# Causal mask of the self blocks' scores: added by VectorE in PSUM instead of laid there by TensorE

## The reference

```python
q = _layernorm(q, qln_g, qln_b) * E ** (-0.25)
k = _layernorm(k, kln_g, kln_b) * E ** (-0.25)
dot = jnp.einsum('bihd,bjhd->bhij', q, k)
causal = jnp.triu(jnp.ones((T, T), dtype=bool), k=1)
dot = jnp.where(causal, -jnp.inf, dot)
att = jax.nn.softmax(dot, axis=-1)
out = jnp.einsum('bhij,bjhd->bihd', att, v).reshape(B, T, E)
```

## Time and profile before

| | |
|---|---|
| Time, median of 3 runs | 1171.24 us (1169.45 to 1173.36) |
| Profiled execution: its time | 1169.33 us |
| Profiled execution: its span | 1167.6 us |
| PE busy | 1029.7 us (88%) |
| DVE busy | 724.1 us (62%) |
| ACT busy | 596.7 us (51%) |
| POOL busy | 267.0 us (23%) |
| Row maxima on DVE (L1158) | 256 instructions, 270.1 us |
| Mask strips on PE (L521) | 1024 matmuls, 18.9 us of busy time |

### The profile page before, as it was taken

How to read it: one execution, slowest core, us unless ns; L and a number is a source line. 1 busy time by engine, 2 the same in 40 slices (tenths; PEclk the granted TensorE clock), 3 DMA queues, 4 the chain that set the end, 5 groups by cost and what they waited for, 6 DMA issues and landing times.

```text
span 1167.6 us, 29067 instructions
## 1 busy us (share of the span) xinstructions
PE 1029.7 (88%) x10925; PEld 767.3 (66%) x10925; DVE 724.1 (62%) x1584; ACT 596.7 (51%) x1024; POOL 267.0 (23%) x309
## 2 busy tenths in 40 slices
PE   6899999999999999999999999877189999999930
PEld 3556666666666666666666666545179999999930
DVE  4656666666677877677878787753524444444446
ACT  3567767767755566665555655654122222222225
POOL 1053232232232200000212121132512222222210
PEclk9999999999999999999999999998589999999975
DMA  7117446446441000100101100011267777677656
GB/s 290 29 36 249 149 144 209 147 146 211 142 126 30 12 20 12 47 12 20 40 26 35 34 26 30 13 40 40 92 203 215 219 215 210 213 214 218 202 201 253
DMA packets 95078, 139.25 MB, mean 119 GB/s; under 512 B 11264, under 2 KB 68992, under 8 KB 93920
## 3 DMA queue, kind: packets, MB, share of 16 engines
q1 hardware_dynamic: 88320, 114.98, 31.6%
q0 software_dynamic: 6624, 22.42, 4.9%
HBM read 76.56 MB, written 60.29 MB: 117 GB/s over the span
## 4 chain that ended last, share of the span: by engine, by line
PE 80%; issue 6%; DVE 5%; ACT 3%; DMA 2%; SPq 2%; another core or an unknown queue 0%; ACTq 0%; DVEq 0%; POOLq 0%
PE PS L824 11%; PE PS L561 11%; PE PS L835 11%; PE PS L582 10%; PE PS L531 5%; PE PS L635 5%; PE PS L639 5%; PE PS L706 5%; PE PS L653 4%; PE PS L680 3%; PE PS L538 2%; PE PS L669 2%; PE PS L534 2%; ACT pT L904 2%; PE PS L813 1%
## 5 line engine op out<-in xcount | busy, mean ns | idle before, releaser
L1158 DVE TENSOR_REDUCE part<-PS 128x6 f32<-128x768 f32 (+1 forms) x256 | 270.1, 1087 | 117.9 <-PE PS L538 85.0
L904 ACT ACTIVATE pT<-PS 128x768 f32<-128x768 f32 (+1 forms) x256 | 220.8, 915 | 102.6 <-PE PS L561 89.8
L561 PE MATMUL PS<-big 32*128 32x256 f32 (+1 forms) x2048 | 133.2, 373 | 20.4 <-issue 11.7
L1595 POOL TENSOR_SCALAR_AFFINE_SELECT pT<-pT 128x512 f32<-128x512 f32 x128 | 84.2, 659 | 278.7 <-ACT pT L904 274.9
L824 PEld LDWEIGHTS PS<-oT,big 128*128 128x128 f32 x1136 | 139.8, 194 | 5.4 <-ACT oT L1034 1.8
L824 PE MATMUL PS<-oT,big 128*128 128x128 f32 x1136 | 140.6, 278 | 1.0 <-ACT oT L1034 1.0
L561 PEld LDWEIGHTS PS<-big 32*128 32x128 f32 x2048 | 95.9, 184 | 62.5 <-issue 61.2
L582 PE MATMUL PS<-pT,vaug 128*32 128x256 f32 (+1 forms) x2048 | 125.0, 361 | 13.6 <-DVE sq L1227 3.5
L835 PE MATMUL PS<-w2s,qkn 128*128 x568 | 134.5, 380 | 0.0
L1034 ACT ACTIVATE oT<-PS 128x256 f32<-128x256 f32 x71 | 27.2, 383 | 192.7 <-PE PS L813 192.7
L1615 POOL DMA_INDIRECT xs_dram<-rows_all,posi x64 | 62.1, 971 | 250.1 <-PE PS L531 174.2
(11 more groups left out here) (170 smaller groups left out, 1533.8 us busy)
## 6 DMA issues: line engine op xcount, KB each, us to landing
big<-w SPq DMA_DIRECT2D x71, 512.0 KB
xs_dram<-zrow SPq DMA_DIRECT2D x24, 1496.0 KB, 9.8
oT<-xs_dram SPq DMA_DIRECT2D x71, 136.0 KB
xin<-xT SPq DMA_DIRECT2D x16, 256.0 KB, 2.9
w2s<-w POOLq DMA_DIRECT2D x1, 4096.0 KB, 15.8
xb<-x SPq DMA_DIRECT2D x16, 256.0 KB, 11.2
xin<-ctxT SPq DMA_DIRECT2D x16, 256.0 KB, 2.8
big<-nmaxT SPq DMA_DIRECT2D x128, 4.0 KB
```

The lines of the kernel that those rows point to most:

```text
L561: ins = pe.matmul(o, keys, a[r0:r1, 0, g, q0:T], start=True, stop=True)
L904: act.activation(pT[:, k % 2, 2 * half:2 * half + 2, 0:wide], src, ACT.Exp).then_inc((exp_a, exp_b)[half], 1)
L1158: dve.tensor_reduce(dst, src, AX.X, ALU.max, negate=True).then_inc((max_a, max_b)[half], 1)
L1595: pool.affine_select(d, d, [[0, 2], [0, 2], [1, P]], ALU.is_ge, 0.0, base=0, channel_multiplier=-1).then_inc(masked, 1)
```

## The change

The strips go. TensorE scores self groups like cross groups (`start=True`), and VectorE adds a mask tile `causal` (128x128, fp32, in SBUF) in place onto the diagonal squares in PSUM, one instruction of 128x512 elements for two banks, two for a group, before it takes the maxima. A new semaphore `veiled` counts the adds; each reduction waits for the add of its own half. Both adds stand ahead of the first reduction.

```diff
@@ decoder_block
         ident = sb("ident", [P, P])
-        identb = sb("identb", [P, P], BF16)
-
-        strips = sb("strips", [P, STRIPS, P], BF16)
+
+        causal = sb("causal", [P, P])
...
@@ score(u), TensorE
-                if not cross:
-                    if k == 0:
-                        pe.wait_ge(mask_ready, 1)
-                    for j in range(STRIPS):
-                        for i in range(GRP):
-                            r0, r1 = PADDED * i, PADDED * (i + 1)
-                            diagonal = bank(S_BANK[i])[:, 0:2 * T].rearrange("p (t k) -> p t k", t=2)
-                            pe.matmul(diagonal[:, :, PADDED * j:PADDED * (j + 1)], strips[r0:r1, j, :],
-                                      identb[r0:r1, r0:r1].unsqueeze(1).to_broadcast([PADDED, NT, PADDED]),
-                                      start=(j == 0), stop=False, skip_group_check=True)
...
-                            ins = pe.matmul(o, q, a[r0:r1, 1, g, 0:P], start=False, stop=True,
-                                            skip_group_check=True)
+                            ins = pe.matmul(o, q, a[r0:r1, 1, g, 0:P], start=True, stop=True)
...
@@ TensorE, before the quarters
-            pe.wait_ge(mask_laid, 1)
-            for j in range(STRIPS):
-                ins = pe.transpose(bank(5)[:, j * P:(j + 1) * P], columns4[:, j, :], ident[:])
-            ins.then_inc(mask_pe, 1)
@@ VectorE, before the quarters
-            for i in range(GRP):
-                ins = dve.tensor_copy(columns4[:, :, PADDED * i:PADDED * (i + 1)],
-                                      cst[:, 1, :].rearrange("p (j m) -> p j m", j=STRIPS))
-            ins.then_inc(mask_laid, 1)
...
-            dve.tensor_copy(identb[:], cst[:, 0, :])
+            dve.tensor_copy(causal[:], cst[:, 1, :]).then_inc(veiled, 1)
...
-            dve.wait_ge(mask_pe, 1)
-            dve.tensor_copy(strips[:].rearrange("p j q -> p (j q)"), bank(5)).then_inc(mask_ready, 1)
@@ maxima(u, half), VectorE
                 if half == 0:
                     dve.wait_ge(scores_pe, NG * n + g + 1)
...
+                    if not crossed(n):
+                        if g == 0 and n == 0:
+                            dve.wait_ge(veiled, 1)
+                        for both in S_HALF:
+                            own = both.rearrange("p (i b k) -> p i b k", i=2, k=P)[:, :, 0:3:2, :]
+                            dve.tensor_tensor(own, own, causal[:].unsqueeze(1).unsqueeze(1).to_broadcast([P, 2, 2, P]),
+                                              ALU.add).then_inc(veiled, 1)
+                if not crossed(n):
+                    dve.wait_ge(veiled, 2 * (NG * n + g) + half + 2)
                 src = S_HALF[half].rearrange("p (i c) -> p i c", i=2)
```

More of the change, by code:

```diff
@@ L27 @@
 PADDED = 32
-STRIPS = P // PADDED
 MASKED = -1e30
@@ L260, in decoder_block @@
         wm = pflat[:, 2816:2816 + 64]
-        columns4 = pflat[:, 3072:3072 + 4 * P].rearrange("p (j t) -> p j t", j=STRIPS)
         PS = ctx.enter_context(nc.psum_tensor("PS", [P, 4096], F32))
@@ L273, in decoder_block @@
         ident_ready, centered = sem("ident_ready"), sem("centered")
-        mask_laid, mask_pe, mask_ready = sem("mask_laid"), sem("mask_pe"), sem("mask_ready")
+        veiled = sem("veiled")
         init_link, pool_ready, zrow_ready = sem("init_link"), sem("pool_ready"), sem("zrow_ready")
@@ L533, in score @@
                             o = bank(S_BANK[i])[:, 0:P]
-                            ins = pe.matmul(o, q, a[r0:r1, 1, g, 0:P], start=False, stop=True,
-                                            skip_group_check=True)
+                            ins = pe.matmul(o, q, a[r0:r1, 1, g, 0:P], start=True, stop=True)
                         else:
                             o = bank(S_BANK[i])[:, P:P + T]
-                            ins = pe.matmul(o, q, a[r0:r1, 1, g, :], start=False, stop=True,
-                                            skip_group_check=True)
+                            ins = pe.matmul(o, q, a[r0:r1, 1, g, :], start=True, stop=True)
                 ins.then_inc(scores_pe, 1)
```

## The result

The changed kernel takes 1234.9 us (median of 4 runs, 1225.5 to 1236.7), against 1170.4 for the kernel before in the same series (4 runs, 1169.5 to 1173.4): a ratio of 1.053, with a 95% interval from 1.0472 to 1.0589. The forecast was 1230, slower by 5%. In the profiled executions, on which the sum was made, it is 1233.21 against 1169.33: 63.9 us more, where the sum gave 59.0.

What follows compares the result with a forecast made beforehand. TensorE was taken to bound the kernel, with `score_T` waiting for VectorE's `max_a`. Adds cost 67.3 us, strips give back 8.3, net 59.0 on 1169.33: 1228.3, forecast 1230 us, 5% slower; range 1215 to 1255.

Steps and rivals of the forecast that it cites:

- The place: In self groups, `score_T` needs `max_a`; adds ahead of the first reduction delay that reduction by 1.22 us.
- The price of an add in PSUM: VectorE's mask adds, 128x512: 0.69 us each, starts 0.61 us apart, taken from an add that reads PSUM.
- Rival 1: Adds dearer than a PSUM read: 1.48 us a pair gives 1246 us, 2.4 us about 1303; chance 0.14.
- 2.28 us to `score_T`: From the start of the first add to `score_T`: 1.22 plus 1.06 us, in all four kinds of quarter.
- Quarters 14 to 71: Delay of `score_T`: 36.6 us for 30 quarters without slack, 12.9 with r = 2, 12.0 with r = 3.
- The strips: Removing 16 strip matmuls in each of 64 groups brings scores 0.13 us earlier per group, 8.3 us off.
- Rival 3: VectorE's added work is hidden at the wait for `max_a`, only the strips' removal shows: 1163 us; chance 0.02.
- Rival 4: Strips held TensorE 0.29 us a group, not 0.13: 1220 us; chance 0.07, shared with some missed slack.
- Quarters 8 to 13: Next scores wait for `max_b` in quarters 8 to 12, 4.6 us more; quarter 13 waits for the reduction, 1.2.
- quarter 12: The 128x512 projection at half clock covers the adds' delay there, so it was put at nothing.
- rival 2: TensorE's clock falls after longer waits: 1 to 2 us early, 14 for a dip per block (1244); chance 0.08.
- the prediction's own sign of being wrong there: The forecast counts as wrong if TensorE's clock dips between 60 and 400 us.

Runs made afterwards that it cites:

- The two fitted fills: Idle 128x256 matmuls before quarter 14: 19 in the changed kernel (1223.1 us, 1.0535), 10 in it without adds or mask under the maxima (1156.04 us, 0.9953).
- the first profile: The profiled execution of the changed kernel, 1233.21 us, against 1169.33 us for the kernel before.
- the second profile: The changed kernel run once more, unaltered, as yardstick for later runs: 1227.31 us, ratio 1.0569 to the kernel before.

## Why the prediction was right

**The place.** Right. The adds' 1.2 us arrive in `score_T` in every quarter; taking them off that way gives back 25 us or more even with the collision in it, and doubling them adds 1.19 per quarter.

**The price of an add in PSUM.** Right: 694 ns and starts 0.61 apart, against 0.69 taken from the read. Rival 1 falls. Its milder price, 1.48 us for a pair, came from a mean that mixes two cases: the 741 ns of L1234 are 26 instructions of 0.68 to 0.69 us and 6 that took 0.86 to 1.12. The reduction starts 1.21 us after the first add, not 1.38, as it would if each instruction waited for the end of the one before. The section of the Trainium skill that the prediction sets against this, "VectorE: DVE Perf Modes", "The DRAIN you can't avoid", itself adds that a next instruction that is not held starts earlier; the rows agree with that.

**2.28 us to `score_T`.** It is 2.26 in all four kinds. The steps on the way were each 0.02 us too large and cancel in a quarter: the pair of adds costs 1.20 instead of 1.22, and the strips give back 0.11 instead of 0.13. That they cancel is luck. VectorE is busy 75.5 us more, not 89: the 128 adds are 88.8 us one by one, but 83.0 as time covered, and the reductions overlap the rest.

**Quarters 14 to 71.** 61.5 us of the sum less 58 times 0.13 for the strips is 54.0; measured 54.2. The block is 3.70 longer, as forecast. (VectorE was busy 64% of this stage before, not the 60 that the prediction names; no term hangs on it.)

**The strips.** Right in the changed kernel, where VectorE's wait is the last in all four kinds and the strips count in each. As a worth of the removal alone, 8.3 us is too much: with r = 2 and 3 a wait for ScalarE covers it, which the prediction didn't see (it named the transpose alone), and 0.11 in each of 30 quarters is 3.3. Rival 3's 1163 us was therefore 4 to 5 too low, had the adds been free. Rival 4 falls.

**Quarters 8 to 13.** This is the mis-sized term: 4.6 + 1.2 - 6 x 0.13 = 5.0 us forecast, 8.7 measured. The two fitted fills are at full clock both, with the adds and without: 27.7 and 21.3 us, 6.4 apart, where the sum had 4.6 + 1.2 = 5.8. So the waits were sized well, but for quarter 12, which was put at nothing and costs 0.8 at full clock. What was left out of the sum is the half clock: 31.7 - 27.7 = 4.0 us in the first profile, 29.6 - 27.7 = 2.0 in the second. Some 0.7 of the first is the dip in quarter 8, which began before any add. This is rival 2, at the start of the run. In the steady quarters of the profile that the sum was made for it didn't come: the clock stayed 1.00 between 60 and 400 us. In the second profile it did, once, at quarter 16 (2.1 us), so the prediction's own sign of being wrong there, a dip between 60 and 400 us, is met by that run; its price is small.

**The rest.** The last 1.8 us, behind quarter 71, are not explained; the runs of one kernel differ by more.

## What to carry to other kernels

Judge work moved onto an engine by the wait that ends last at its place, not by the engine's share of busy time: 83 us on an engine that was busy 62% cost 64. Look next at what slides along with it, since an instruction that is shifted by half a microsecond can meet one on another engine and take three to seven times as long. And price long waits, of a start-up phase above all, twice, once for the wait itself and once for the clock that TensorE may have behind it.

## What was unexpected of the hardware

- A VectorE instruction of 128x66 with two inputs in SBUF, 0.22 us alone, took 0.64 to 1.20 us beside GpSimd's mask or sum, and ended just behind it. A 128x2 one took 1.14 instead of 0.16. Adds with one input in PSUM kept theirs (0.69 alone, 0.70 beside GpSimd).
- An add of 128x512 in place in PSUM costs no more than one from PSUM into SBUF (694 and 692 ns).
- Waits of 0.66 to 1.54 us ahead of `score_T` left the granted clock at 2.4 GHz from 100 to 400 us in both profiles of the changed kernel. Yet waits of 1.54, 1.54 and 1.01 us in quarters 14 to 16 were followed by 6.8 us at 1.2 GHz in one of them, and waits of 1.16 and 0.69 us in one quarter by 3.4 us in 5 of the 14 blocks with the adds between the reductions. With waits of 1.85 to 2.73 us the clock fell again and again (mean 0.83 to 0.88), which cost some 60 us in the kernel with the adds twice.
